# One 128-row product for gate and value in the second mixture's experts, and the 320/192 split of the B product in the two LSTM scans

## What is computed

```
def step(h, inp):
    dt_t, B_t, C_t, u_t = inp
    dA = jnp.exp(dt_t[..., None] * A)
    h = dA * h + (dt_t * u_t)[..., None] * B_t[:, None, :]
    y = jnp.einsum('bcn,bn->bc', h, C_t)
    return (h, y)
```

```
g = xt @ wih.T + h @ whh.T + bih + bhh
i, f, gg, o = jnp.split(g, 4, axis=-1)
c = sigmoid(f) * c + sigmoid(i) * tanh(gg)
h = sigmoid(o) * tanh(c)
```

```
h = silu(einsum('ecd,edh->ech', buf, w1)) * einsum('ecd,edh->ech', buf, w3)
y = einsum('ech,ehd->ecd', h, w2)
```

## Time and profile before

| what | value |
| --- | --- |
| median of 3 runs | 2707.17 us (2706.18 to 2713.07) |
| the profiled execution's own time | 2733.23 us |
| its span, first to last instruction | 2731.2 us |
| mean granted TensorE clock | 0.816 of 2.4 GHz |
| PE busy | 2162.6 us (79%) |
| DVE busy | 1484.7 us (54%) |
| POOL busy | 1180.4 us (43%) |
| ACT busy | 985.8 us (36%) |
| LSTM scans (layers 1 and 2) | from 1784 to 2028 us and from 2124 to 2367 us |
| experts of mixture 2 | 2547 to 2680 us |

### The profile page before, as it was taken

How to read it: one execution, slowest core, us unless ns; L and a number is a source line. 1 busy time by engine, 2 the same in 40 slices (tenths; PEclk the granted TensorE clock), 3 DMA queues, 4 the chain that set the end, 5 groups by cost and what they waited for, 6 DMA issues and landing times. The chain is left out here.

```text
span 2731.2 us, 41623 instructions
## 1 busy us (share of the span) xinstructions
PE 2162.6 (79%) x14854; PEld 1444.8 (53%) x14854; DVE 1484.7 (54%) x3188; ACT 985.8 (36%) x2290; POOL 1180.4 (43%) x1121
## 2 busy tenths in 40 slices
PE   6999977899999767497665777689986899864692
PEld 4666644677778655397321223255552555543351
DVE  2433348755655023121368986878868788633352
ACT  2212212344444321043256664745446454300110
POOL 3111012744445501300406996179971899613104
PEclk7565558999999875599777999789997899955896
DMA  5000011111111100184002221022210222100562
GB/s 210 0 0 0 0 41 20 42 25 33 33 33 33 38 5 12 44 228 136 25 15 53 83 77 43 2 74 73 72 39 2 71 72 70 40 7 18 151 195 75
DMA packets 195919, 149.62 MB, mean 55 GB/s; under 512 B 93287, under 2 KB 155059, under 8 KB 194210
## 3 DMA queue, kind: packets, MB, share of 16 engines
q1 hardware_dynamic: 191138, 138.49, 18.1%
q0 software_dynamic: 4608, 8.86, 1.1%
HBM read 108.68 MB, written 39.19 MB: 54 GB/s over the span
## 5 line engine op out<-in xcount | busy, mean ns | idle before, releaser
L1567 DVE TENSOR_TENSOR_SCAN mc_states<-psum,mc_dbu 128x512 f32<-128x512 f32 x384 | 459.4, 1217 | 47.8 <-issue 30.1
L1477 POOL TENSOR_TENSOR mc_hc<-mc_states,mc_c_sb 128x1024 f32<-128x1024 f32 x192 | 451.7, 2352 | 45.0 <-DVE mc_states L1567 37.6
L1605 PE MATMUL psum<-mc_hc,ident 128*128 128x512 f32 x768 | 414.5, 636 | 52.4 <-POOL mc_hc L1477 52.4
L1488 ACT ACTIVATE psum<-dt,a 128x508 f32<-128x508 f32 x384 | 261.7, 687 | 20.1 <-DVE mc_states L1567 19.2
L1467 POOL TENSOR_TENSOR mc_dbu<-dtu,mc_b_sb 128x512 f32<-128x512 f32 (+1 forms) x192 | 227.1, 1184 | 13.0 <-ACT mc_b_sb L1495 13.0
L636 POOL TENSOR_TENSOR fw_tmp<-zeros 128x30 f32<-128x30 f32 (+14 forms) x240 | 121.4, 506 | 255.0 <-DMA zeros<-fw_blocks 236.9
L1605 PEld LDWEIGHTS psum<-mc_hc,ident 128*128 128x128 f32 x768 | 123.5, 192 | 117.7 <-POOL mc_hc L1477 75.3
L189 POOL TENSOR_TENSOR t_rstd<-t_var,neg_half 128x4 f32<-128x4 f32 x32 | 32.3, 1009 | 291.7 <-DVE t_var L51 291.7
L640 POOL TENSOR_TENSOR zeros<-zeros,fw_tmp 128x30 f32<-128x30 f32 (+14 forms) x240 | 133.3, 556 | 18.8
L1553 DVE TENSOR_TENSOR mc_dbu<-psum,dtu 128x512 f32<-128x512 f32 (+1 forms) x192 | 136.7, 712 | 7.3 <-PE psum L1582 7.0
L1495 ACT ACTIVATE mc_b_sb<-psum 128x256 f32<-128x256 f32 (+1 forms) x192 | 70.1, 365 | 171.5 <-PE psum L1588 170.6
(11 more groups left out here) (394 smaller groups left out, 4724.5 us busy)
## 6 DMA issues: line engine op xcount, KB each, us to landing
mc_c_sb<-c_rows SPq DMA_DIRECT2D x192, 256.0 KB, 3.2
e_w<-in_L_ffn_ew SPq DMA_DIRECT2D x64, 256.0 KB, 3.1
slots_x<-zeros SPq DMA_DIRECT2D x12, 1024.0 KB, 12.6
e_x<-slots_x SPq DMA_DIRECT2D x96, 128.0 KB, 2.3
slots_y<-e_y SPq DMA_DIRECT2D x96, 128.0 KB, 1.9
e_w<-in_L_ffn_w SPq DMA_DIRECT2D x64, 128.0 KB, 2.3
fw_blocks<-fw_A SPq DMA_DIRECT2D x128, 32.0 KB, 1.7
zeros<-fw_blocks SPq DMA_DIRECT2D x8, 512.0 KB, 3.7
```

The costliest lines, as they stand in the source:

```text
L1477: nc.gpsimd.tensor_tensor(hc[:, k % 2], states[:, k % 2], c_sb[:, k % AHEAD, :].unsqueeze(1).to_broadcast([P, HALVES, GT]), ALU.mult).then ...
L1488: nc.scalar.activation(decay4[:, f, :, 1:P], z["dt"][:, f, cols].rearrange("p (b t) -> p b t", b=GS)[:, :, 1:P], ACT.Exp, scale=z["a"][:, ...
L1567: nc.vector.tensor_tensor_scan(out=states[:, k % 2, f, :], data0=decay_ps[:, f, :], data1=dbu[:, k % 2, f, :], initial=0.0, op0=ALU.mult, ...
L1605: last = nc.tensor.matmul(y_ps[:, f, :], m.ident, hc[:, k % 2, f, :], start=False, stop=(n == NSTATE - 1), skip_group_check=True)
```

## The change

Two edits. In the scans SPLIT becomes 320 in all three layers, so in layers 1 and 2 the part of the B product on DVE grows from 256 to 320 columns and the part that goes over ACT and POOL shrinks from 256 to 192. In the experts, w1 and w3 are used as one stationary operand of 128 columns: one product writes the gate to partitions 0 to 63 and the value to partitions 64 to 127 of a PSUM bank. ACT's silu reads partitions 0 to 63 and writes partitions 64 to 127 of `act1`; DVE multiplies both on partitions 64 to 127 and writes partitions 0 to 63 of `gated`.

```diff
-    SPLIT = GT - (256 if lstm else 192)
+    SPLIT = GT - 192
...
-        act1 = sb("e2_act1", [H2, 2, SLOT_TILE])
+        act1 = sb("e2_act1", [P, 2, SLOT_TILE])[H2:2 * H2]
...
-        up_ps = [m.bank[2 + u][0:H2, :].rearrange("p (k c) -> p k c", k=2) for u in range(2)]
+        up_ps = [m.bank[2 + u][:, 0:SLOT_TILE] for u in range(2)]
...
-                        nc.scalar.activation(act1[:, u, :], up_ps[u][:, 0, :], ACT.Silu).then_inc(s["silu_done"], 1)
+                        nc.scalar.activation(act1[:, u, :], up_ps[u][0:H2, :], ACT.Silu).then_inc(s["silu_done"], 1)
...
-                    nc.vector.tensor_tensor(gated[:, k % 2, :], act1[:, k % 2, :], up_ps[k % 2][:, 1, :], ALU.mult).then_inc(s["gated_done"], 1)
+                    nc.vector.tensor_tensor(gated[:, k % 2, :], act1[:, k % 2, :], up_ps[k % 2][H2:2 * H2, :], ALU.mult).then_inc(s["gated_done"], 1)
...
-                    for n in range(2):
-                        last = nc.tensor.matmul(up_ps[k % 2][:, n, :], ws[:, k, n * H2:(n + 1) * H2], xT[:, k, :], start=True, stop=True)
-                    last.then_inc(s["up_mm"], 1)
+                    nc.tensor.matmul(up_ps[k % 2], ws[:, k, 0:2 * H2], xT[:, k, :], start=True, stop=True).then_inc(s["up_mm"], 1)
```

## The result

| | before | changed |
| --- | --- | --- |
| median of 4 runs | 2706.68 us (2705.85 to 2713.07) | 2737.58 us (2735.96 to 2743.55) |
| profiled execution | 2733.23 us | 2735.96 us |
| ratio | | 1.0113, 95% interval 1.0091 to 1.0135 |

What follows compares the result with a forecast made beforehand. It took POOL to bound most scan turns, PE those after chunk ends and the expert turns. Scans -16.8 and experts -6.7 made -23.5 us, from 2707.2 to 2683.7 us, range 2674 to 2698.

Steps and rivals of the forecast that it cites:

- The scans' sum: Layers 1 and 2: ordinary turns fall to PE's 3.32 us (POOL 3.26, DVE 3.23), gaining 17.6 us, net 16.8.
- a term beside it: Chunk ends: longer B product ahead of `finish` costs 0.14 us in 6 places, 0.8 us; clock allowance 4 us either way.
- the wait for the tanh: Scans, before `parts`: 0.17 us waiting for ACT, claimed to hide DVE's 0.14 us longer product, with 0.12 to spare.
- The experts' chain: Experts: transposes, copy, gating product, contracting product set the turn at 1.90 us, 0.11 less over about 61 turns, -6.7 us.
- the unseen operation: Experts: reading one half of the partitions and writing the other; bounded by nothing or 0.02 us, 1.2 us in all.
- The step that failed: Experts: PE idling some 0.3 us a turn leaves the clock alone, as layer 0's scan has 0.97 with less PE work.
- the rule set against the row: Experts: the skill page says repeated short idle times make the clock swing; part or all of the gain would be lost.
- The rival on the other side: Experts: new idle times drop TensorE to 1.2 GHz, 0.64 us more a turn, +39 us, total 2729; chance 0.06.
- About half of the loop: Experts: share of the loop at half clock from which the slower-clock case decides, 46 us at stake, 23.5 to be lost.

Runs made afterwards that it cites:

- split alone: Only the scans' SPLIT changed against the kernel before, experts as before: 2693.45 against 2705.09 us, ratio 0.9952.
- the fill: The scans' split without the experts' edit, plus eight unread small products on PE while it waits for `finish` at chunk ends: 2682.22 against 2700.89 us, ratio 0.9924.
- the halves exchanged: Experts' edit with its product made twice, plus w3 and w1 exchanged so only ACT's silu reads the upper half: ratio 0.9984 against before, loop 125.7 us.
- the gating product first: Experts' edit, old split, with DVE's gating product ahead of the next copy of slots: 2684.51, 2687.83, 2734.11 and 2747.02 us against 2705.09.
- 1 KB pieces: The gating product first, plus each partition moving slots in one 1 KB piece instead of two of 512 bytes: ratio 1.0134 against before.

## Why the prediction was wrong

**The scans' sum was right, a term beside it too small.** POOL's limit went, the longer DVE product disappeared in the wait for the tanh, and the turn is 3.32. The eight stretches between chunk ends lost 17.0 us, by the trace, where 17.6 were forecast. The chunk ends cost 5.2 us more (49.3 against 44.1 for the six), where the sum had 0.8 and the range 4 either way. All of them are now long in both traces that have this split and nothing else at the chunk ends (changed, split alone), and none is once PE is kept busy there. That the clock falls for PE's idle time for `finish` is shown by the fill. Why it is now all six is not: before, the same wait of 1.84 us cost the clock at three ends and not at the other three. A chunk now lasts 49.8 to 50.1 and 8.1 to 8.3 us every time, so each end may meet the clock in the state of the one before, but I did not test it.

**The experts' chain was right, one link too short.** A turn of 1.90 needs the gating product to overlap the copy. The sum took 0.34 from a row where both start at partition 0 and bounded the unseen operation by 0.02 us, the difference in its own length. Its real price was in its neighbours: 0.12 us before it and 0.12 behind it. Only the one before lies on the chain: 0.47 to the copy, 0.46, the product 0.42, 0.06 to PE and 0.64 are the 2.05 measured, 0.12 + 0.02 + 0.01 above the 1.90. With the halves exchanged the chain would allow the 1.90; the 1.91 measured there is PE's time too. PE's own turn is 1.44, not 1.58: the wider operand starts 0.10 us earlier, and the product that went is worth 0.47 (1.00 with two, 0.53 with one), not 0.43.

**The step that failed** is this sentence of the prediction: "The rows say that this leaves the clock alone". It compared busy times, 45.06 of 60 us in layer 0's scan at clock 0.97 with 1.58 of 1.90 in the new turn. That column cannot decide it: the changed kernel's first turns have 4.89 of 6.50, the same share, and lost the clock, and at half clock PE is busy 110.00 of 110.00 in one kernel without getting it back. Recorded matmuls overlap (the transposes of 2511.46 last 0.44 us, the next product starts at 2511.74), so a busy PE in that column can be one that does little. And the 0.97 itself held a fall: 1.00 up to the chunk end at 1579, 0.81 in its 9 us and 1.00 behind it. What the runs showed in its place: with one product of 256 columns less per turn the granted clock was 0.50 for all but nearly 7 us of the loop, and in the traces with that product or a smaller one put back it rose to 1.00 and stayed. Which property of PE's work the clock answers to stays open. The right direction was that of the rule set against the row, on short idle times between groups (the Trainium skill, TensorE: Matmul & The Clock Gate, "A second HAM failure mode"), but the case is harder than the rule: it reports a clock that swings, and here it fell once and stayed down for the 166 us that were left of the loop.

**The rival on the other side** described what came, and was given 0.06. Its price was too low, too: it took PE's work at half clock, 2.65 a turn, and forgot that the chain grows with it. At half clock transposes to copy take 0.73 us (2518.98 - 2518.25) instead of 0.47 and the contracting product 1.15 (2521.06 - 2519.91) instead of 0.64, while DVE's steps stay at 0.45 and 0.42, 2.81 in all, so 45 us instead of 39 in the experts. "About half of the loop" as the point of decision was of no use, since the loop is at one clock or the other nearly as a whole.

## What to carry to other kernels

Before a product is taken out of a loop on TensorE, ask what the loop's clock lives on. A loop that PE bounds at full clock may owe the clock to the very work that is dropped, and then the change costs several times what it was to save (45 us instead of a gain of 7). Look at the granted clock of the changed loop, not at busy time, and over several executions; taking away the wait that opens behind the dropped work was not enough by itself (two of four executions). When data moves to another half of the partitions, price the neighbours of the instruction, and give the crossing to an engine whose turn has room (ACT here).

## What the runs showed of the hardware that was not expected

- The same loop has two steady states: 1.44 to 2.1 us a turn at full clock or 2.62 at half clock. The first was traced with the gating product first and the second in its version with 1 KB pieces; one program had executions of 2684.51 and 2747.02 us, with mean clocks of 0.823 and 0.791.
- Products of 512 columns ran for 5 us at half clock and then at full, where 110 us of the experts' own products without a pause at half clock did not.
- Products of 0.2 us a turn that nobody reads, or of 2 us at a chunk's end, were free or nearly so and kept the 44 us of the experts' clock in three executions of four and brought back 7 us at the chunk ends.
- A DVE instruction of 256 elements whose inputs start at partition 64, among others that start at 0, lost 0.12 us of overlap on each side; with all at 0 none.
